# Experts' weights in twelve portions of two pieces instead of six portions of four, in the first stage of a transformer block

## What is computed

```
x = x + conv_attention(layer_norm(x))   # 1x1 conv to q, k, v; 3x3 depthwise conv;
                                        # channel attention in 8 heads; 1x1 conv
t = tokens(x)                           # 16384 tokens of 192
t = t + moe(layer_norm(t))              # top 2 of 4 experts:
                                        # h = gelu(x @ w1[e] + b1[e]); y = h @ w2[e] + b2[e]
```

## Time and profile before

| | |
|---|---|
| median of three runs | 1994.67 us (1994.42 to 1999.99) |
| span of the profiled execution, first to last instruction | 1993.4 us, no time of its own is listed; the median is 1.3 us longer |
| first stage, by the first instruction behind it | 619.1 us |
| mean granted clock of TensorE, share of full speed | 0.966 |
| busy over the span | PE 92%, PEld 75%, DVE 69%, ACT 64%, POOL 56% |

### The profile page before, as it was taken

The page is one execution under the profiler, slowest core; times in us unless marked ns, Lnnn a source line. Parts: engine busy times, 40 slices in busy tenths (PEclk is TensorE's granted clock), DMA queues, the critical chain, the costliest instruction groups (busy, mean ns, idle before and its releaser), DMA issues.

```text
span 1993.4 us, 36026 instructions
## 1 busy us (share of the span) xinstructions
PE 1838.7 (92%) x9782; PEld 1502.9 (75%) x9782; DVE 1379.8 (69%) x3382; ACT 1277.2 (64%) x2468; POOL 1123.5 (56%) x1079
## 2 busy tenths in 40 slices
PE   5799999999795989898999999999999999999956
PEld 3566666666564767688989989899898888888844
DVE  3789999999777474667676686776766655555532
ACT  3688888888674435465666666666667667676622
POOL 3666666666663015476767676767677676344320
PEclk9899999999896999899999999999999999999977
DMA  3453323333333798777788878788787877656569
GB/s 97 147 148 93 92 89 93 92 91 92 99 111 95 228 290 275 263 221 216 211 229 215 227 213 228 213 229 224 216 226 195 242 204 202 171 155 180 129 184 338
DMA packets 254367, 361.97 MB, mean 182 GB/s; under 512 B 27396, under 2 KB 183940, under 8 KB 254212
## 3 DMA queue, kind: packets, MB, share of 16 engines
q1 hardware_dynamic: 191556, 278.59, 46.3%
q0 software_dynamic: 50880, 60.59, 15.0%
q10 hardware_dynamic: 11776, 20.98, 3.0%
HBM read 222.76 MB, written 137.30 MB: 181 GB/s over the span
## 4 chain that ended last, share of the span: by engine, by line
PE 57%; DMA 4%; DVE 3%; POOL 2%; issue 2%; ACT 1%; SPq 1%; POOLq 0%; DVEq 0%; ACTq 0%
PE bank L1804 21%; PE bank L1820 14%; PE bank L1787 7%; PE bank L1821 6%; PE bank L1847 4%; DMA xn<-acc_scratch 3%; PE bank L1839 3%; POOL xs_scratch L1251 1%; POOL acc_scratch L1266 1%; PE bank L1869 1%; DMA acc_scratch<-yo,tix 1%; DMA xs<-xs_scratch 0%; PE bank L1872 0%; DVE hl L1758 0%; ACT L1319 0%
## 5 line engine op out<-in xcount | busy, mean ns | idle before, releaser
L1266 POOL DMA_INDIRECT acc_scratch<-yo,tix x268 | 439.0, 1638 | 304.2 <-DVE yo L1647 238.0
L1804 PE MATMUL bank<-x_all,w1b 128*128 128x512 f32 x2010 | 548.8, 402 | 1.0 <-ACT hf L1319 1.0
L1820 PE MATMUL bank<-w_hl,hh 128*128 x1608 | 495.5, 360 | 6.7 <-DVE hl L1758 5.8
L1319 ACT ACTIVATE hf<-bank,b_col 128x512 f32<-128x512 f32 x402 | 276.7, 688 | 335.5 <-PE bank L1804 335.4
L1758 DVE TENSOR_TENSOR hl<-hf,hh 128x512 fp32r<-128x512 f32 x402 | 277.2, 690 | 272.5 <-ACT hh L1322 272.3
L1821 PE MATMUL bank<-w_hl,hl 128*128 x1608 | 404.9, 252 | 0.0
L1804 PEld LDWEIGHTS bank<-x_all,w1b 128*128 128x128 f32 x2010 | 348.2, 188 | 55.1 <-ACT hf L1319 1.4
L625 DVE SCALAR_TENSOR_TENSOR bank<-zwin,wdw,bank 128x512 f32<-128x512 f32 (+2 forms) x462 | 336.3, 734 | 43.4 <-PE bank L731 34.8
L1820 PEld LDWEIGHTS bank<-w_hl,hh 128*128 128x128 f32 x1608 | 302.1, 188 | 40.9 <-issue 10.4
L1821 PEld LDWEIGHTS bank<-w_hl,hl 128*128 128x128 f32 x1608 | 306.1, 190 | 17.4
L1251 POOL DMA_INDIRECT xs_scratch<-xn,idx x256 | 262.2, 1024 | 85.1 <-issue 75.7
(11 more groups left out here) (261 smaller groups left out, 2902.3 us busy)
## 6 DMA issues: line engine op xcount, KB each, us to landing
w1b<-w1s_scratch SPq DMA_DIRECT2D x134, 768.0 KB, 5.1
xs<-xs_scratch SPq DMA_DIRECT2D x67, 522.0 KB, 6.0
xtok_scratch<-xtok SPq DMA_DIRECT2D x32, 384.0 KB, 2.7
v_scratch<-zv SPq DMA_DIRECT2D x64, 192.0 KB
vc_scratch<-yo ACTq DMA_DIRECT2D x64, 192.0 KB, 4.5
vd<-vc_scratch SPq DMA_DIRECT2D x64, 192.0 KB
xtok<-xtok_scratch SPq DMA_DIRECT2D x32, 384.0 KB, 7.3
acc_scratch<-x SPq DMA_DIRECT2D x32, 384.0 KB, 5.5
```

What stands on the lines that cost most here:

```text
L1266: nc.gpsimd.indirect_dma_start(acc_dram, bass.IndirectOffsetOnAxis(ap=tix[:, J % 4, t:t + 1], axis=0), yo[:, J % YN, t, :], None, compute_ ...
L1319: nc.scalar.activation(hf[:, k % 3, :], lb[k % 2][:, :], ACT.Gelu, bias=b1_col[:, bass.ds(exp_of[J] * CH + k, 1)]).then_inc(gelu, 1)
L1804: last = nc.tensor.matmul(lb[k % 2][:, :], w[:, q, :], v[:, J % 2, :], start=(i == 0), stop=(i == 4))
L1820: nc.tensor.matmul(yb[t][:, 0:2 * C], hh[:, k % 3, cols], w, start=(k == 0), stop=False, skip_group_check=True)
```

## The change

The number of static steps grows from 15 to 23: the loop now runs from step 7 to step 20 in 7 turns, before from 5 to 26 in 11. Pieces are made two at a time, in steps 1 to 4, 21 to 24, 27, 28, 30 and 31. The second load moves from step 3 to step 5, the third from 29 to 25, the last from 31 to 29. POOL makes all low parts.

```
-            FIRST, LAST, LO, HI = -2, NB + 2, 5, NB - 6
+            FIRST, LAST, LO, HI = -2, NB + 2, 7, NB - 12
...
-            PIECES_AT = {1: (0, 4), 2: (4, 8), NB - 5: (8, 12), NB - 4: (12, 16), NB - 2: (16, 20), NB: (20, 24)}
-            LOAD_AT = {0: 0, 3: 1, NB - 3: 2, NB - 1: 3}
+            PIECES_AT = {i: (2 * k, 2 * k + 2) for k, i in enumerate((1, 2, 3, 4, NB - 11, NB - 10, NB - 9, NB - 8, NB - 5, NB - 4, NB - 2, NB - 1))}
+            LOAD_AT = {0: 0, 5: 1, NB - 7: 2, NB - 3: 3}
...
-                    for n, g in pieces_of(i) if not (i.static and i.val == NB) else []:
+                    for n, g in pieces_of(i):
                         pool.wait_ge(e_hi, n + 1)
...
-                    if i.static and i.val == NB:
-                        for p, g in pieces_of(i):
-                            dve.wait_ge(e_hi, p + 1)
-                            dve.wait_ge(e_lo, p)
-                            hi, lo, raw = pieces[p]
-                            nc.vector.tensor_tensor(lo, raw, hi.bitcast(FP32), ALU.subtract).then_inc(e_lo, 1)
```

## The result

The changed kernel takes 1969.52 us (median of four runs, 1968.95 to 1969.9), the kernel before on the same chip 1995.17 (four runs, 1994.42 to 1999.99). The ratio is 0.9866, 95% interval 0.985 to 0.9882. The prediction was 1968.7, with a range of 1965.5 to 1974.5, and faster with a chance of 0.96.

A forecast was written before the change was run, and what follows sets the result against it. PE was taken to bound the first stage's loop periods, with four periods lengthened behind portions of pieces. The terms summed to -25.93 us, from 1994.67 to 1968.7 us, with a range of 1965.5 to 1974.5.

The forecast's parts named there:

- The ring's wait: Periods 3 and 29: ACT no longer waits for stores before rewriting a piece buffer; -12.05 and, with pairs of `w2`, -9.98 us.
- the smaller terms: Periods 2 and 28: two pieces instead of four exceed ACT's slack by less; -0.80 and -0.46 us.
- The slack of ACT: ACT has 0.82 us spare behind a step's end; a pair costs only the excess, 0.05 (`w1`) or 0.38 (`w2`).
- The rival without slack: Each pair costs its whole ACT time, 0.82 more in ten periods, 8.2 us in all: 1976.9 us; chance 8%.
- Eight static steps: Periods 5, 6 and 21 to 26 leave the loop; a static period takes 0.12 us more: +0.96 us.
- six further pairs: Periods 4, 5 and 22 to 25 get a pair of pieces ahead of them, 0.05 us each: +0.30 us.
- Period 31: Two pieces of `w2` instead of four: 1.19 us less ACT delay and 1.6 from PE's clock staying up; -2.8 in all.
- The end of the stage: DVE's four subtractions go: POOL's tap and scaling end 0.85 us earlier, PE's 0.28 wait for DVE's tap goes; together -1.1.
- Loads: The last load, issued in step 29, is read some 16 us later, against 7.76 us needed before; the others have longer.
- The rival with a wait for a load: The last load takes over twice its 7.76 us, ACT stands behind step 30 some 10 us: 1978.7 us; chance 3%.

The follow-up runs named there:

- The ring of eight: The kernel before with eight buffers in the ring of `wph` and `wpl` instead of four, still four pieces a step; 1977.32 us, ratio 0.9903.
- the ring of two: The changed kernel with two buffers in the ring of `wph` and `wpl` instead of four; 2023.35 us, ratio to the kernel before 1.0134.
- Doubling the pair: The changed kernel with every high part made twice on ACT, first into a spare tile that nothing reads; 1982.08 us, ratio 0.9929.
- the pair on DVE: The changed kernel with its last pair of pieces moved to step 32 and its low parts made on DVE; 1970.19 us, ratio 0.9865.
- the one on POOL: The changed kernel with its last pair of pieces moved to step 32 and its low parts made on POOL; 1970.05 us, ratio 0.9871.

## Why the prediction was right, by its steps

*The ring's wait* (-12.05 in period 3, and most of -9.98 in period 29). Measured -12.06 and -10.02; the smaller terms, -0.80 in period 2 and -0.46 in period 28, came out at -0.83 and -0.50. The ring of eight takes the same waits away by another edit, the ring of two brings them back: shown. The step that mattered most was to read the queue's positions: when SP issues the stores and when ACT needs the buffer again.

*The slack of ACT* (0.05 for a pair of `w1`, 0.38 for one of `w2`). Periods 22 to 25 are 16.92 to 16.95 against 16.87 to 16.91 of the static ones without a pair ahead of them; periods 28 and 29 are 17.24, 0.33 over period 27. Doubling the pair adds 0.81 to 0.85 to the periods of `w1`, about the 0.83 of two more copies (they start 0.41 to 0.42 apart): once the slack is used, added work costs its whole length. That is shown. The rival without slack is out.

*Eight static steps* (+0.96) and *six further pairs* (+0.30). Periods 4 to 6 and 21 to 26 together grew by 1.13 against the 1.26 forecast. Why a written-out step takes longer was not known when it was priced and is not known now; the price came from rows, and held.

*Period 31* (-2.80). Measured -2.84. The division was right as well: 1.19 for ACT, measured 1.17, and 1.6 for the clock, measured 1.67. The clock fell behind the pause of before in all four traces of the kernel before and its variants with these pieces (19.52 to 19.58), so there was a fall to be rid of. But that is not a rule: behind the same pause it did not fall in the three runs with four pieces in the changed kernel, and what decides it is open. The prediction had no reason for this part beyond the length of the pause, and without a fall in the kernel before the term would have been 1.2.

*The end of the stage* (-1.1). Measured 27.67 - 26.24 = -1.43, the one term that was mis-sized. POOL's tap and scaling gave 3.53 - 2.70 = 0.83 (0.85 forecast). The end of the scaling at 606.86 that the forecast starts from stands in no row; by its row it is 605.17 + 1.66 = 606.83, which makes 0.82. Behind it I took only the wait of 0.28, the idle time in brackets; since PE's rows overlap, that wait cost 0.47, and the stretch to PE's last products became 0.48 shorter. The rest up to the next stage became 0.11 shorter, for which I have no cause. That DVE's subtractions were on the path mainly by POOL's slowing, and not by their own length, is shown by the pair on DVE (1.13 longer, where the two subtractions take 2.50) against the one on POOL.

*Loads.* No pair waits for one. The rival with a wait for a load is out.

The terms sum to -26.54 from the end of step 1 on, against -25.93. In the profiled execution that end came 1.02 later than before (62.14 against 61.12), which no edit touches; in the traces of the experiments it lies between 60.00 and 61.91. So the stage ends 25.52 earlier, 593.60 instead of 619.12, and behind it nothing moved (25.6 over the span). That the span came within 0.3 us of the forecast (1967.8 against 1967.5) is in part chance: the terms by themselves were 0.61 off.

## What to carry to other kernels

A buffer that is written again in the next step has only that step for its store, and the store's time counts from where its queue issues it, not from where the data is ready; giving it one step more, by a longer ring or by spreading the work, was worth the whole stall here. Where one engine bounds a loop, price its stall with its clock: six waits of 6.0 to 7.4 us cost 8.0 to 9.1 each here. Work on an engine that is not the bound cost what exceeded its slack at that place of the step (0.82 us here), so look for the place where that engine waits anyway. And the idle time in front of a row of PE can understate what a wait costs, since its rows overlap (0.28 in brackets, 0.47 in time).

## What was not expected of the hardware

PE's clock fell behind 9 of 17 pauses of the same length, 2.13 to 2.23 us, at a price of 1.63 (19.52 - 17.89) to 1.74 us (20.12 - 18.38) each, and in periods 28 and 29 of one code it fell in the one in one run and in the other in the next. A written-out step without pieces took 16.87 to 16.91 (the one behind the loop of a single turn 17.27), one in a loop of 7 or 11 turns 16.75 to 16.80, one in a loop of a single turn 16.89 to 16.90. POOL's addition of two 128x512 tiles took 1.73 instead of 1.29 beside DVE's subtraction of two tiles in SBUF. The Trainium skill ("SBUF — State Buffer", SBUF: two separate sides) states that of a GpSimd operation that reads SBUF and a DVE operation with two inputs in SBUF, the one that starts first holds their shared ports for its whole instruction and the other is blocked. Here the first subtraction still had 577.70 + 2.50 / 2 - 577.86 = 1.09 us to go when the addition began, and the addition took 0.44 longer; so the trace agrees that the two disturb each other, and not that the later one waits for the whole of the other.
